# Two conditioned linear-attention layers: scores in column groups of 32, z on two engines, the output bias as a product

## The chip, the cores and the metric

The kernel runs on one core of a Trainium2 chip. The core has a matrix engine (PE in the profile; PEld is its loading of stationary operands), three engines that work on rows of 128 partitions (DVE, ACT, POOL) and a queue for transfers (SP; ACT issues some too). Each engine works through its own list of instructions in order, and the lists meet only at semaphores. The metric is the time of one execution on the device in microseconds (us), and of several executions the median.

## What is computed

Two layers, each on 16 sequences of 256 rows and 256 features. Layer 0 has 8 heads of 32 features and layer 1 has 16 heads of 16; they differ also in how a mask is applied. Cut to what matters, a layer is:

```python
xn = layernorm(x, w, b)
q = softmax(xn @ Wq + bq, over the features of a head)
k = softmax(xn @ Wk + bk + mask, over the 256 rows)
v = (xn @ Wv + bv) * mask
att = einsum('bnhd,bnhl->bhdl', k, v)        # a d x d block for each head: the "scores" of the kernel
y = einsum('bnhd,bhdl->bnhl', q, att)
h = layernorm(y) * (1 + scale) + shift       # scale and shift from the condition
x = x + silu(h) @ W_out + b_out
```

## The kernel before

**Tiling.** An item is one sequence of one layer, so there are 32 items, numbered through both layers. Rows lie on partitions: a sequence is a tile of 128 x 512 (T = 2 halves of 128 rows, each of 256 features), and features are cut into C = 2 chunks of 128. Pairs of buffers alternate by the item's parity.

**The stages of an item.**
- z: DVE takes mean and variance of x (`x_statistics`, `x_aggregate`), POOL the reciprocal root (`x_scale`), DVE writes z = (x - mean) * rstd in two halves of 128 x 256 (`x_normalise`, L933). ACT makes z_hi in 16 bits (L397), adding Z_SCALE as a bias, DVE the rest z_lo (L944). Two DMA transposes turn both.
- products: PE makes K transposed (`project_k`, L1375, 12 products of 256 columns) and Q and V (`project_qv`, L1395, 12 of 512 columns).
- softmax: DVE and ACT. exp(k) is turned on PE (L1409), exp(q) too (L1439).
- scores: `attend` (L1467). G = 64: for each chunk and half of the rows, two products of 128 rows with 64 x 64 columns in 32-bit floats, one for each half of the array's columns; 8 products an item. Off-diagonal head blocks come out too. `att_scale` (DVE, L1020 and L1022) multiplies them by `block_mask`, which sets them to zero.
- y: `attention_out` (L1483), 8 products an item with 64 rows each, 66 or 68 columns wide (the last column of each head gives the sum of exp(q)). DVE divides and takes statistics; POOL and ACT normalise one half each (L707, L469). PE turns the result (L1450), ACT conditions it (L483), ACT and DVE make silu in two 16-bit parts g_hi and g_lo (L505, L1094).
- out: `project_out` (L1428), 12 products of 256 columns. POOL has written x_plus = x + b_out (L719), and DVE adds the product to it and writes x (`residual`, L1102).

**Order.** Everything is written out by hand: each engine's function lists the stages of different items one after the other, with a loop for the middle of the program. In PE's loop one turn holds these stages, each of another item: y, scores, out, exp(q) turned, Q and V, exp(k) turned, y turned, K. A wait stands ahead of a stage where a buffer must be full or free.

**Tiles of the array.** A product is laid on a part of PE's array that its shape gives. The profile prints it as rows*columns: 128*128 for the projections, 64*128 for `attention_out`, 128*64 for `attend`.

## Time and profile before

| | us |
|---|---|
| median of 3 runs | 308.25 |
| lowest and highest of them | 308.12, 308.55 |
| the profiled execution, whole | 307.67 |
| its span, first to last instruction | 305.9 |
| PE busy | 287.3 |
| DVE busy | 281.4 |
| ACT busy | 234.2 |
| POOL busy | 152.7 |

The profile has a page and a trace. The page sums each engine's busy time and follows the chain of work that ended last backwards from the last instruction. The trace can be asked for the busy times in a stretch of the span, for groups of equal instructions, and for single instructions in order of time. A record of PE lasts longer than PE is held by it, because products run through the array one behind the other; what a product costs a full PE is the time from its start to the next start. The same holds for the other engines to a smaller degree. Products of 32-bit floats have two records each, the turns on PE one.

### The profile page before, as it was taken

What the parts mean: (1) busy time and instruction counts of PE and PEld (TensorE: products, weight loads), DVE (VectorE), ACT (ScalarE), POOL (GpSimd) and SP (SyncE); (2) the same over time, 40 slices, a digit from 0 to 9 for tenths busy, and PEclk for the clock granted to TensorE, in tenths of its full rate; (3) what the DMA queues carried; (4) which work ended last, traced back from release to release, by engine and by line L of the source; (5) the groups of instructions that cost most, each with busy time, mean ns of one, the idle gap of its engine ahead of it and who ended that gap; (6) DMA issues with size and microseconds to landing.
All of it is one profiled execution on the core that took longest, in us unless ns stands there. A gap on an engine that the chain in (4) does not pass through costs nothing.

```text
span 305.9 us, 8521 instructions
## 1 busy us (share of the span) xinstructions
PE 287.3 (94%) x2629; PEld 210.3 (69%) x2629; DVE 281.4 (92%) x850; ACT 234.2 (77%) x525; POOL 152.7 (50%) x268
## 2 busy tenths in 40 slices
PE   8388999999999999999999999999999999999665
PEld 3145666677777777777777777777777777777553
DVE  3967899999989999999999999999999999888985
ACT  1426347698998888888898989998889988888760
POOL 1220202335555555666655655555556665564774
PEclk9869999999999999999999999999999999999998
DMA  7499856553222222211221222232222222711224
GB/s 222 134 252 264 197 130 168 128 155 56 55 53 54 55 51 49 48 39 43 55 53 37 55 54 51 54 56 51 51 43 50 52 40 54 239 36 38 70 69 139
DMA packets 51485, 26.73 MB, mean 87 GB/s; under 512 B 36656, under 2 KB 49648, under 8 KB 51440
## 3 DMA queue, kind: packets, MB, share of 16 engines
q1 hardware_dynamic: 50000, 25.03, 33.6%
q10 hardware_dynamic: 1440, 1.15, 1.1%
q8 instruction: 22, 0.36, 0.5%
q14 instruction: 23, 0.19, 0.2%
HBM read 13.55 MB, written 4.23 MB: 58 GB/s over the span
## 4 chain that ended last, share of the span: by engine, by line
PE 85%; DVE 6%; DMA 3%; issue 2%; ACT 1%; ACTq 0%; SPq 0%; DVEq 0%
PE ps_qv L1395 25%; PE ps_eo L1428 14%; PE ps_k L1375 14%; PE ps_y L1483 11%; PE ps_att L1467 6%; PE ps_qy L1439 5%; PE ps_eo L1409 4%; PE ps_qy L1450 4%; DMA m1r<-in_mask_row 2%; DMA zt_hi<-z_hi 2%; PE ps_k L1428 1%; DVE w_raw L817 1%; DVE g_lo L1094 1%; PE ps_y L1333 1%; DVE z_lo L944 1%
## 5 line engine op out<-in xcount | busy, mean ns | idle before, releaser
L719 POOL TENSOR_TENSOR x_plus<-x_all,row_b 128x512 f32<-128x512 f32 x32 | 43.2, 1354 | 53.5 <-DVE x_all L1102 53.5
L1395 PE MATMUL ps_qv<-w_hi,zt_hi 128*128 128x512 f16 x128 | 49.0, 383 | 0.0
L1395 PE MATMUL ps_qv<-w_lo,zt_hi 128*128 128x512 f16 x128 | 48.9, 382 | 0.0
L1395 PE MATMUL ps_qv<-w_hi,zt_lo 128*128 128x512 f16 x128 | 48.8, 381 | 0.0
L679 POOL TENSOR_SCALAR x_ve<-x_mv 128x2 f32<-128x2 f32 x32 | 6.2, 193 | 75.5 <-DVE x_mv L921 75.3
L1375 PE MATMUL ps_k<-zt_hi,w_hi 128*128 128x256 f16 x128 | 35.4, 277 | 7.9 <-DVE w_lo L830 5.9
L1428 PE MATMUL ps_eo<-wo_hi,g_hi 128*128 128x256 f16 x120 | 33.4, 278 | 3.7 <-DVE x_all L1102 2.4
L1483 PEld LDWEIGHTS ps_y<-att_e,eq_t 64*128 64x128 f32 x512 | 31.1, 187 | 7.0 <-issue 7.0
L1483 PE MATMUL ps_y<-att_e,eq_t 64*128 64x66 f32 (+1 forms) x512 | 35.6, 278 | 0.3 <-DVE att_e L1022 0.3
L408 ACT ACTIVATE ek<-k_neg,k_neg_max 128x256 f32<-128x256 f32 x64 | 31.6, 497 | 5.1 <-DVE k_neg_max L956 5.1
L1375 PE MATMUL ps_k<-zt_hi,w_lo 128*128 128x256 f16 x128 | 35.5, 277 | 0.0
L1375 PE MATMUL ps_k<-zt_lo,w_hi 128*128 128x256 f16 x128 | 35.5, 277 | 0.0
L1094 DVE SCALAR_TENSOR_TENSOR g_lo<-g,g_hi 128x512 f16<-128x512 f32 x32 | 34.1, 1066 | 1.5 <-ACT g_hi L505 1.4
L483 ACT ACTIVATE h<-ps_qy,item_col 128x256 f32<-128x256 f32 x64 | 32.4, 558 | 3.0 <-DVE g L1085 2.4
L440 ACT ACTIVATE v<-ps_qv,item_col 128x256 f32<-128x256 f32 x64 | 29.6, 467 | 6.5 <-PE ps_qv L1395 5.4
L1428 PE MATMUL ps_eo<-wo_hi,g_lo 128*128 128x256 f16 x120 | 33.3, 277 | 0.0
L1428 PE MATMUL ps_eo<-wo_lo,g_hi 128*128 128x256 f16 x120 | 33.2, 276 | 0.0
L459 ACT ACTIVATE eq_t<-ps_qy 128x512 f32<-128x512 f32 x32 | 19.1, 596 | 18.0 <-PE ps_qy L1439 17.9
L397 ACT ACTIVATE z_hi<-z,z_plus 128x512 f16<-128x512 f32 x32 | 22.8, 714 | 5.5 <-DVE z L933 5.4
L450 ACT ACTIVATE eq<-q_sub 128x512 f32<-128x512 f32 x32 | 19.8, 620 | 8.5 <-DVE q_sub L1000 8.4
L1102 DVE SCALAR_TENSOR_TENSOR x_all<-ps_eo,x_plus 128x512 f32<-128x512 f32 x30 | 20.1, 669 | 5.5 <-PE ps_eo L1428 4.8
L990 DVE TENSOR_REDUCE q_max<-ps_qv 128x16 f32<-128x512 f32 (+1 forms) x32 | 21.1, 660 | 4.1 <-ACT v L440 4.1
(101 smaller groups left out, 755.1 us busy)
## 6 DMA issues: line engine op xcount, KB each, us to landing
m_row<-mask_rows SPq DMA_DIRECT2D x32, 128.0 KB, 3.3
out<-x_all SPq DMA_DIRECT2D x16, 256.0 KB, 2.2
wemb<-in_w_emb SPq DMA_DIRECT2D x2, 1024.0 KB, 7.1
w_raw<-in_w_in SPq DMA_DIRECT2D x2, 768.0 KB, 5.2
x_all<-in_x SPq DMA_DIRECT2D x3, 512.0 KB, 5.2
x_all<-in_x SPq DMA_DIRECT2D x2, 768.0 KB, 6.3
x_all<-in_x ACTq DMA_DIRECT2D x4, 256.0 KB, 5.9
row_b<-in_rows SPq DMA_DIRECT2D x2, 384.0 KB, 6.3
```

The costliest lines, as they stand in the source:

```text
L397: nc.scalar.activation(z_hi[p][:, :], z[p][:, :], ACT.Identity, bias=z_plus[:, 0:1]).then_inc(z_hi_ready, 1)
L408: last = nc.scalar.activation(part(ek[p], c), part(k_neg[p], c), ACT.Exp, scale=-1.0, bias=k_neg_max[p][:, c:c + 1], accum_out=k_sum[p][:, ...
L440: nc.scalar.activation(part(v[p], t), ps_qv[:, t * BANK + D:(t + 1) * BANK], ACT.Copy, scale=item_col[a.layer][:, m:m + 1]).then_inc(v_rea ...
L483: last = nc.scalar.activation(part(h[p], c), part(ps_qy, c), ACT.Identity, scale=item_col[a.layer][:, ab + 2 * c:ab + 2 * c + 1], bias=ite ...
L719: pool.tensor_tensor(x_plus[p][:, :].rearrange("p (t f) -> p t f", t=T), sequence_of(a).rearrange("p (t f) -> p t f", t=T), row_b[a.layer] ...
L990: vec.tensor_reduce(q_m, q, AX_X, ALU.max).then_inc(q_max_ready, 1)
L1094: vec.scalar_tensor_tensor(g_lo[p][:, :], g[p][:, :], G_SCALE, g_hi[p][:, :], ALU.mult, ALU.subtract)\
L1102: vec.scalar_tensor_tensor(sequence_of(a), out_bank(a)[:, :], 1.0 / OUT_SCALE, x_plus[p][:, :], ALU.mult, ALU.add).then_inc(x_new, 1)
L1375: last = mm(part(ps_k, d).rearrange("p (t s) -> p t s", t=T), w[l][:, c * W + d * P:c * W + (d + 1) * P], zz[p][:, :].rearrange("p (t c s) ...
L1395: last = mm(part(ps_qv, t, BANK), zz[p][:, (t * C + c) * P:(t * C + c + 1) * P], w[l][:, c * W + D:(c + 1) * W], start=(n == 0), stop=(n = ...
L1428: last = mm(part(out_bank(a), t), gg[p][:, c * S + t * P:c * S + (t + 1) * P], part(w[l], c), start=(n == 0), stop=(n == 3 * C - 1))
L1483: last = mm(ps_y[:, at:at + E], eq_t[p][r * G:(r + 1) * G, c * S + t * P:c * S + (t + 1) * P], att_e[l][p][r * G:(r + 1) * G, c * E:(c + 1 ...
```

## The change

- **Scores.** G becomes 32. `attend` makes 16 products of 32 x 32 columns, one for each quarter of the array's columns, in place of 8 of 64 x 64. `att_scale` writes each score block four times over, side by side, times a mask of 128 columns, so that att_e is a full 128 x 128 block diagonal per chunk (two instructions of 128 x 128 elements). `attention_out` then is 4 products of 128 rows and 132 or 136 columns in place of 8 of 64 rows and 66 or 68 columns, and y lies half by half.
- **z.** z = x * rstd + shift, with Z_SCALE inside the shift. DVE makes the first half, ACT the second. POOL's `x_scale_and_shift` has four small instructions in place of two. z_hi is a plain copy in 16 bits, z_lo a plain difference.
- **Bias.** x_plus and POOL's sum are gone. Each half of `project_out` begins with a product of 33 rows: row 0 of `bias_pair` holds b_out's high part, row 32 the low part, the rows between are zero. It starts the sum in PSUM, and the 6 products follow. `residual` adds to x itself.
- **Start.** The mask rows of items 0 and 1 are loaded straight from the input. Loads of x move from ACT's queue to SP's, `mask0_row` and `mask1_row` behind others on ACT's. PE begins with Q and V of item 0, then K. SP's waits for buffers are ordered anew, and stores stand in the loop.
- **Order.** The lists of all engines are written anew, with the same stages.

```diff
-    G = 64
-    GROUPS = P // G
-    GH = [G // d for d in DH]
+    HC = [P // d for d in DH]
+    G = 32
...
             load_sequence(0)
             load(ident[:, :], identity, ident_in)
+            load_sequence(1)
+            load(head_ind[:, :], indicators, ind_in)
             load(m0r[:, :], mask0_row, mask_in)
             load(m1r[:, :], mask1_row, mask_in)
-            load(head_ind[:, :], indicators, ind_in)
-            for b in range(1, 4):
-                load_sequence(b)
...
+            def x_normalise(a):
+
+                j, p = a.index, a.parity
+                act.wait_ge(x_shift_ready, j + 1)
+                if not a.first_two:
+
+                    act.wait_ge(z_lo_ready, j - 1)
+                nc.scalar.activation(part(z[p], 1), part(sequence_of(a), 1), ACT.Identity, scale=x_rstd[p][:, 1:2],
+                                     bias=x_shift[p][:, 1:2]).then_inc(z_ready[1], 1)
...
-                nc.scalar.activation(z_hi[p][:, :], z[p][:, :], ACT.Identity, bias=z_plus[:, 0:1]).then_inc(z_hi_ready, 1)
+                nc.scalar.activation(z_hi[p][:, :], z[p][:, :], ACT.Copy).then_inc(z_hi_ready, 1)
...
                 pool.tensor_scalar(x_ve[p][:, :], x_mv[p][:, 1:2 * T:2], Z_SCALE ** -2, EPS * Z_SCALE ** -2, ALU.mult, ALU.add)\
-                    .then_inc(x_ve_ready, 1)
-                pool.wait_ge(x_ve_ready, j + 1)
-                pool.tensor_tensor(x_rstd[p][:, :], x_ve[p][:, :], neg_half[:, :], ALU.pow).then_inc(x_rstd_ready, 1)
+                    .then_inc(x_powered, 1)
+                pool.wait_ge(x_powered, 3 * j + 1)
+                pool.tensor_tensor(x_rstd[p][:, :], x_ve[p][:, :], neg_half[:, :], ALU.pow).then_inc(x_powered, 1)
+                pool.wait_ge(x_powered, 3 * j + 2)
+                pool.tensor_tensor(x_nm[p][:, :], x_mv[p][:, 0:2 * T:2], x_rstd[p][:, :], ALU.mult).then_inc(x_powered, 1)
+                pool.wait_ge(x_powered, 3 * j + 3)
+                pool.tensor_scalar(x_shift[p][:, :], x_nm[p][:, :], -1.0, Z_SCALE, ALU.mult, ALU.add).then_inc(x_shift_ready, 1)
...
-            def add_out_bias(a):
...
-                pool.tensor_tensor(x_plus[p][:, :].rearrange("p (t f) -> p t f", t=T),
-                                   sequence_of(a).rearrange("p (t f) -> p t f", t=T),
-                                   row_b[a.layer][:, bo:bo + D].unsqueeze(1).to_broadcast([P, T, D]), ALU.add)\
-                    .then_inc(x_plus_ready, 1)
...
-                for t in range(T):
-                    last = vec.tensor_scalar(part(z[p], t), part(sequence_of(a), t), x_mv[p][:, 2 * t:2 * t + 1],
-                                             x_rstd[p][:, t:t + 1], ALU.subtract, ALU.mult)
-                last.then_inc(z_ready, 1)
+                vec.tensor_scalar(part(z[p], 0), part(sequence_of(a), 0), x_rstd[p][:, 0:1], x_shift[p][:, 0:1],
+                                  ALU.mult, ALU.add).then_inc(z_ready[0], 1)
...
+                for c in range(C):
+                    att = part(ps_att, c, G)
+                    if l == 0:
+                        last = vec.scalar_tensor_tensor(scaled[:, c], att.unsqueeze(1).to_broadcast([P, P // G, G]),
+                                                        k_rsum[p][:, c:c + 1], mask, ALU.mult, ALU.mult)
...
                 for t in range(T):
+                    here = part(out_bank(a), t)
+                    mm(here, bias_ones[:, :], bias_pair[l][:, :], start=True, stop=False)
                     n = 0
...
-                        for r in range(GROUPS):
+                        for r in range(P // G):
...
                 for t in range(T):
                     for c in range(C):
-                        for r in range(GROUPS):
-                            at = r * BANK + (t * C + c) * E
-                            last = mm(ps_y[:, at:at + E], eq_t[p][r * G:(r + 1) * G, c * S + t * P:c * S + (t + 1) * P],
-                                      att_e[l][p][r * G:(r + 1) * G, c * E:(c + 1) * E], start=True, stop=True)
+                        last = mm(ps_y[:, t * BANK + c * E:t * BANK + (c + 1) * E], eq_t[p][:, c * S + t * P:c * S + (t + 1) * P],
+                                  part(att_e[l][p], c, E), start=True, stop=True)
```

Where the instructions stand now is shown at two places of PE's list and one of POOL's. In a row stand the line, the operation, what it writes and reads, and the size of what it writes; x8 stands for so many alike in a row.

PE in the loop of layer 1, before: y of one item directly ahead of the scores of the next, and then the first half of an out product.

```order
L1375 MATMUL ps_k<-zt_hi,w_lo 128x256
L1483 MATMUL ps_y<-att_e_1,eq_t 128x66 x8
L1467 MATMUL ps_att<-ek_row,v 64x64 x8
L1428 MATMUL ps_eo<-wo_hi,g_hi 128x256
L1428 MATMUL ps_eo<-wo_lo,g_hi 128x256
```

Here `ps_eo` is the bank that out and the turned exp(k) share. PE after, the same stages: y, then out with its product of 33 rows (L1501) ahead of each half.

```order
L1515 MATMUL ps_qy<-ident,eq 128x128 x4
L1557 MATMUL ps_y<-att_e_1,eq_t 128x136 x4
L1501 MATMUL ps_eo<-bias_pair,bias_ones 128x256
L1506 MATMUL ps_eo<-wo_hi,g_hi 128x256
L1506 MATMUL ps_eo<-wo_lo,g_hi 128x256
L1506 MATMUL ps_eo<-wo_hi,g_lo 128x256
L1506 MATMUL ps_eo<-wo_hi,g_hi 128x256
L1506 MATMUL ps_eo<-wo_lo,g_hi 128x256
L1506 MATMUL ps_eo<-wo_hi,g_lo 128x256
L1501 MATMUL ps_eo<-bias_pair,bias_ones 128x256
L1506 MATMUL ps_eo<-wo_hi,g_hi 128x256
```

Y has moved away from the scores, and out has two products more. In the built program the tile of L1501 is 64*128, since 33 rows are more than 32 and at most 64; its neighbours on both sides are 128*128. PE after, at the end of the same turn of the loop, where the scores stand now, between K and the turned y.

```order
L1449 MATMUL ps_k<-zt_hi,w_lo 128x256
L1543 MATMUL ps_att<-ek_row,v 32x32 x16
L1526 MATMUL ps_qy<-ident,y_z 128x128 x4
L1469 MATMUL ps_qv<-w_hi,zt_hi 128x512
L1469 MATMUL ps_qv<-w_lo,zt_hi 128x512
```

The scores are the one stage left on 128*32 tiles; y is on 128*128 now.

POOL in the loop, before: one turn with x_plus (L719).

```order
L692 TENSOR_SCALAR y_ve<-y_mv 128x2
L693 TENSOR_SCALAR y_nm<-y_mv 128x2
L695 TENSOR_TENSOR y_rstd<-y_ve,neg_half 128x2
L697 TENSOR_TENSOR y_shift<-y_nm,y_rstd 128x2
L679 TENSOR_SCALAR x_ve<-x_mv 128x2
L682 TENSOR_TENSOR x_rstd<-x_ve,neg_half 128x2
L707 TENSOR_SCALAR y_z<-y_n,y_rstd,y_shift 128x2x2x64
L719 TENSOR_TENSOR x_plus<-x_all,row_b 128x512
```

POOL after: the same turn, with two small steps more for x and without the sum.

```order
L726 TENSOR_SCALAR y_ve<-y_mv 128x2
L727 TENSOR_SCALAR y_nm<-y_mv 128x2
L729 TENSOR_TENSOR y_rstd<-y_ve,neg_half 128x2
L731 TENSOR_TENSOR y_shift<-y_nm,y_rstd 128x2
L709 TENSOR_SCALAR x_ve<-x_mv 128x2
L712 TENSOR_TENSOR x_rstd<-x_ve,neg_half 128x2
L714 TENSOR_TENSOR x_nm<-x_mv,x_rstd 128x2
L716 TENSOR_SCALAR x_shift<-x_nm 128x2
L740 TENSOR_SCALAR y_z<-y_n,y_rstd,y_shift 128x256
```

POOL's only instruction of 128 x 512 has gone.

## Rows read from the trace of the kernel before

**Rows 1.** The page: span, busy times by engine, and the chain by engine.

```profile
span 305.9 us, 8521 instructions
PE 287.3 (94%) x2629; PEld 210.3 (69%) x2629; DVE 281.4 (92%) x850; ACT 234.2 (77%) x525; POOL 152.7 (50%) x268
PE 85%; DVE 6%; DMA 3%; issue 2%; ACT 1%; ACTq 0%; SPq 0%; DVEq 0%
```

**Rows 2.** Stretches: length, then busy time (instructions) of PE, PEld, DVE, ACT, POOL.

```profile
179.48:262.31 82.83, 82.83 (x801) 63.00 (x800) 81.05 (x236) 74.86 (x170) 47.47 (x78) 1.00 0.24 51
262.31:305.90 43.59, 34.88 (x321) 26.48 (x318) 35.88 (x73) 28.66 (x61) 27.39 (x39) 0.96 0.29 97
```

**Rows 3.** The chain in order of time (start, length): Q and V, ten turns apart.

```profile
179.48 2.59 PE ps_qv L1395 x12
...
262.31 2.59 PE ps_qv L1395 x12
```

**Rows 4.** PE in order of time (start, duration) across y, scores and out.

```profile
167.41 0.27 PE L1375 MATMUL ps_k<-zt_hi,w_lo 128*128 128x256 f16 x1
167.61 1.11 PE L1483 MATMUL ps_y<-att_e,eq_t 64*128 64x68 f32 x16
168.66 0.69 PE L1467 MATMUL ps_att<-ek_row,v 128*64 128x64 f32 x16
169.27 0.28 PE L1428 MATMUL ps_eo<-wo_hi,g_hi 128*128 128x256 f16 x1
169.39 0.27 PE L1428 MATMUL ps_eo<-wo_lo,g_hi 128*128 128x256 f16 x1
```

**Rows 5.** The same scores, the second and the third pair of records first.

```profile
168.76 0.58 PE L1467 MATMUL ps_att<-ek_row,v 128*64 128x64 f32 x14
...
168.82 0.52 PE L1467 MATMUL ps_att<-ek_row,v 128*64 128x64 f32 x12
```

**Rows 6.** PE at the start: 32-bit products on the whole array and on quarters.

```profile
7.66 0.61 PE L1312 MATMUL ps_y<-ident,kb 128*128 128x128 f32 x4
8.10 1.02 PE L1315 MATMUL ps_y<-w_raw,fold 128*128 128x512 f32 x2
...
39.29 0.38 PE L1395 MATMUL ps_qv<-w_hi,zt_lo 128*128 128x512 f16 x1
39.60 1.07 PE L1325 MATMUL ps_y<-wemb,cond_s 128*32 128x512 f32 x8
40.59 0.66 PE L1409 MATMUL ps_eo<-ident,ek 128*128 128x128 f32 x4
```

**Rows 7.** Groups by line, 179.48 to 262.31: count, busy us, mean ns, idle before.

```profile
L1094 DVE SCALAR_TENSOR_TENSOR g_lo<-g,g_hi 128x512 f16<-128x512 f32 x10 | 11.4, 1143 | 0.0
L944 DVE SCALAR_TENSOR_TENSOR z_lo<-z,z_hi 128x512 f16<-128x512 f32 x10 | 6.8, 677 | 0.0
L933 DVE TENSOR_SCALAR z<-x_all,x_mv,x_rstd 128x256 f32<-128x256 f32 x18 | 6.5, 402 | 0.0
L1022 DVE TENSOR_TENSOR att_e<-ps_att,block_mask 128x128 f32<-128x128 f32 x10 | 2.8, 277 | 0.0
...
L483 ACT ACTIVATE h<-ps_qy,item_col 128x256 f32<-128x256 f32 x20 | 10.2, 558 | 0.6 <-DVE g L1085 0.6
L397 ACT ACTIVATE z_hi<-z,z_plus 128x512 f16<-128x512 f32 x10 | 7.1, 713 | 0.0
```

**Rows 8.** Groups of the end, 262.31 to 305.9, and its longest wait of PE.

```profile
L1094 DVE SCALAR_TENSOR_TENSOR g_lo<-g,g_hi 128x512 f16<-128x512 f32 x10 | 10.2, 1031 | 1.5 <-ACT g_hi L505 1.4
L1085 DVE SCALAR_TENSOR_TENSOR g<-th,h 128x512 f32<-128x512 f32 x9 | 7.6, 851 | 0.0
...
PE ps_eo L1428 <- DVE x_all L1102: 2.4, 1, 2.4
```

**Rows 9.** DVE and POOL in order of time, one turn of the loop.

```profile
204.79 1.27 POOL L719 TENSOR_TENSOR x_plus<-x_all,row_b 128x512 f32<-128x512 f32 x1 [2.15 <-DVE x_all L1102]
...
205.39 1.22 DVE L1094 SCALAR_TENSOR_TENSOR g_lo<-g,g_hi 128x512 f16<-128x512 f32 x1
```

920 lines of the change are left out of this document (527 added, 393 removed).

## The prediction

> **What bounds the kernel now.** I read four views in this order: the page, a table of stretches, the chain in order of time, and single instructions of one turn of the loop. The page gives a span of 305.9 us with PE busy 94% and 85% of the last chain on PE [rows 1]. Busy shares alone can't separate PE from DVE (92%), so I take one stretch in which the loop repeats. From 179.48 to 262.31, ten turns, PE has no idle time at all: 82.83 us busy of 82.83. DVE has 81.05 and ACT 74.86 [rows 2]. The chain confirms it: Q and V start at both ends of the stretch [rows 3]. A turn, one item, is therefore 82.83 / 10 = 8.28 us, set by the sum of PE's starts. DVE is close behind with 8.11, so taking work from DVE or POOL alone gains nothing here, while each 0.1 us more on PE costs 3.2 us over 32 items. The end, from 262.31 on, is different: PE is busy 34.88 of 43.59 us [rows 2], and waits once 2.4 us for DVE [rows 8]. There a faster DVE can pay.
>
> **What PE pays now for y and scores.** The last K product starts at 167.41 and the first out product at 169.27 [rows 4]. That is 1.86 us, less 0.11 for the K product itself (169.39 less 169.27 is 0.12 for such a product, of 256 columns in 16 bits, straight after a change of tile): 1.75 us. In it are three gaps where the tile's shape changes: 128*128 to 64*128 takes 167.61 - 167.41 - 0.11 = 0.09 us on top of the product. The scores' first step takes 168.76 - 168.66 = 0.10 us, later steps 168.82 - 168.76 = 0.06 [rows 4, 5], so a 32-bit load after a change costs 0.04 more. From 168.76 six steps of 0.06 lead to the last pair at 169.12 or a little less, its own step ends at 169.17, and out starts at 169.27: the change back costs 0.10. In each step of the scores two records start, one for each half of the array's columns.
>
> **Y after.** Four products of 128 rows, 136 columns in layer 1 and 132 in layer 0, two records each, so eight steps. A 32-bit record of 128 columns on the whole array takes (8.10 - 7.66) / 4 = 0.11 us [rows 6], so these take 0.117 and 0.113: 0.92 us an item. No change of shape stands beside them now.
>
> **Scores after.** Entry 0.09, first load 0.04 to 0.05, eight steps of four records, exit 0.10. The trace has no product this small on quarters, so a step is bounded from both sides. Low: four quarter tiles run at once, and a step is half of 0.06 because the columns are half as many. That four do run at once is in the trace: eight records of 512 columns on 128*32 tiles take 40.59 - 39.60 = 0.99 us [rows 6], where one such record takes 4 x 0.11 = 0.44 us; in fours they need 0.88 and one change. High: PE is held to the number of records, now 0.03 us each, so a step of four takes 0.12. I take the geometric middle, 0.06, which is also the nearest row's own step. Scores: 0.09 + 0.05 + 0.48 + 0.10 = 0.72 us (0.48 to 1.20). Y and scores together: 1.64 us for 1.75, a gain of 0.11 (a gain of 0.35 to a loss of 0.37).
>
> **The bias.** Two products of 256 columns in 16 bits an item: 2 x 0.11 = 0.22 us. Each is on a 64*128 tile between neighbours on 128*128, so out has four changes of shape. A change costs 0.09 on the way to 64*128 and 0.10 on the way back [rows 4]: 0.40 us. Together 0.62 us. The bounds are 0.22, if such a product runs through without a gap, and 0.80, if each of the two also pays the 32-bit load of 0.04 and the product behind it too. I take 0.62, since the row shows the very same pair of shapes.
>
> **PE an item:** +0.62 - 0.11 = +0.51 us, over 32 items +16.3 us (+0.27 to +0.99, that is +9 to +32).
>
> **DVE, POOL, ACT.** POOL's x_plus (1.27 us) runs beside g_lo, and g_lo then takes 1.22 us [rows 9] where an instruction of the same form and size takes 0.68 [rows 7]. Without x_plus DVE regains (1.143 - 0.677) = 0.47 us an item, and half of z, at most 0.40. It pays one more att_e instruction, at most 0.28 [rows 7]. DVE ends near 8.11 - 0.47 - 0.40 + 0.28 = 7.5 us a turn, under PE. In the loop this gain is hidden by PE and worth nothing. ACT gets half of z, at most 0.56 by the row of h [rows 7], on 7.49 busy a turn: about 8.0, under PE's 8.8. POOL has two small steps more and a big one less (4.75 us busy a turn): slack. The new waits on POOL and ACT (for x_shift) hold back z of an item that PE wants a turn and more later. Behind ACT's wait stand h and the turned exp(k); z's statistics were taken some ten DVE instructions earlier, so I cost it at nothing; without that cover it is POOL's two steps, under 1 us, once.
>
> **End.** Ten g_lo of 1.031 and nine g of 0.851 [rows 8] against 0.677 make 3.5 + 1.6 = 5.1 us of DVE; I count 3 of them on the path. PE's extra time in out is in the sum for these items too (ten of them, 6.2 us), but PE is idle 8.7 us there [rows 2], so I take back 1.5.
>
> **Start.** POOL's two extra steps and DVE's wait for a mask load that stands two places further back delay the first z; item 0 and 1's masks no longer pass through DRAM. I cost it at +1 us (-1 to +3); PE's first wait is for weights, which DVE makes in both kernels.
>
> **Sum** on the profiled execution: 307.67 + 16.3 - 3 - 1.5 + 1 = 320.5 us. The median of the runs shown is 0.58 us above that execution: **321 us**.
>
> **Rivals.**
> A. *The product of 33 rows runs without a gap, and the four quarters stream at once.* PE then changes by 0.22 - 0.35 = -0.13 us an item, -4 us; with 3 us from the end the kernel comes to 301, or with the middle price of the scores (+0.11, +3.5 us) to 309. For it: with 64 rows left idle, the hardware might treat rows as masked. Against it: the gap of 0.09 before y is a change of exactly these two shapes. It decides as soon as a bias product with its two changes costs under 0.11 us each. This is the faster side. The Trainium skill, TensorEngine Tiling, Key Properties, says that changing the tiling mode drains TensorE; by this rule A cannot be, and the trace's gaps at all three changes agree (0.09 to 0.10 us). It is the rule that speaks most against this change.
> B. *The scores are held to the number of records.* A step is 0.12, the scores 1.20 us, +0.99 us an item: 307.67 + 31.7 - 3.5 + 0.6 = about 336. For it: a turn now has 32 records in a row that do little work each. Against it: two records start together in each step, and the eight big ones on quarters overlap. The same page, Instruction Overhead, states about 60 cycles for each matmul, so that few columns cost as much as 60; by an estimate from it at 2.4 GHz (25 ns a record) the scores take 0.80 us plus 0.24 and the kernel comes to 331. No run shown here has such a product.
> C. *Another engine sets the turn.* ACT at 8.0 us, if an order of stages makes it wait 0.8 us or more for PE every turn, would stretch the turn beyond 8.8. Its lists are new and this can't be read from the trace: 2 to 6 us more, 325.
>
> **Chances.** Forecast (scores low to middle, four gaps; 311 to 329) 0.62. A 0.17, of which 0.13 falls below the old time, 0.02 beside it and 0.02 above. B 0.15. C 0.06. A measurement can tell 0.2% (0.6 us) from no change; faster 0.14, same 0.03, slower 0.83. The range is 307 to 334: it leaves out most of A's faster side (0.12) and the far end of B (0.07).
>
> **What would show it.** In the loop: turns of about 8.8 us with PE without idle time; four gaps of about 0.09 us in out, around each product of the bias; scores of about 0.7 us with four starts close together; y in 0.92 us; g_lo at about 0.68 us; DVE idle about 1 us a turn, waiting for PE. A is right if the bias product follows after 0.11 us. B is right if the scores take over 1 us. The forecast is wrong altogether if PE has idle time in the loop, since then another engine or an order sets the turn, or if the start is off by more than 3 us.

## The result, and the profile after

| | before | after |
|---|---|---|
| median (lowest to highest), 4 runs each on one chip | 308.19 (307.65 to 308.55) | 313.88 (313.43 to 314.3) |
| profiled execution, span | 307.67, 305.9 | 313.51, 311.7 |
| PE busy, span less PE busy | 287.3, 18.6 | 293.9, 17.8 |
| a turn of the loop, layer 0 and layer 1 | 8.28, 8.28 | 8.60, 8.62 |

The change makes the kernel slower by 5.7 us: ratio 1.0186, 95% interval 1.0162 to 1.021. The direction is the predicted one; the forecast was 12.8 us, more than twice as much. Now and then an execution takes far longer than the others of the same program, also of the kernel before (1005.68 us once, 584 us in two of the four of e8b_sum_beside, 341 us at a granted clock of 0.841 in one of e6_one_bias and one of e15_scores_bias33), for reasons that are open; the ratios leave these out.

The page of the kernel after: span, busy times, and the granted clock in 40 slices. It answers to [rows 1].

```profile
span 311.7 us, 9221 instructions
...
PE 293.9 (94%) x2949; PEld 205.6 (66%) x2949; DVE 269.5 (86%) x846; ACT 240.4 (77%) x557; POOL 117.2 (38%) x300
...
PEclk9859999999999999999999999999999999999999
```

PE's busy time grew by 6.6 us and DVE's fell by 11.9. The time outside PE's work hardly changed (18.6 and 17.8 us).

Stretches, with columns as in [rows 2] (length, then busy time and count of PE, PEld, DVE, ACT, POOL, then granted clock, DMA share, GB/s). First the kernel before, then after.

```profile
0.00:80.00 80.00, 70.08 (x550) 45.19 (x551) 66.86 (x246) 44.92 (x103) 22.24 (x59) 0.96 0.66 166
80.00:260.00 180.00, 180.00 (x1736) 136.61 (x1736) 177.85 (x531) 159.01 (x358) 103.04 (x171) 1.00 0.23 49
...
280.00:300.00 20.00, 15.05 (x134) 11.75 (x133) 17.73 (x31) 13.36 (x26) 15.47 (x21) 0.92 0.18 61
```

```profile
0.00:80.00 80.00, 66.31 (x581) 42.62 (x581) 65.16 (x237) 46.64 (x111) 27.78 (x79) 0.94 0.69 163
80.00:260.00 180.00, 180.00 (x1885) 129.69 (x1884) 165.00 (x510) 157.08 (x369) 74.69 (x190) 1.00 0.25 51
...
280.00:300.00 20.00, 19.34 (x196) 13.38 (x195) 16.93 (x46) 16.82 (x36) 8.66 (x18) 1.00 0.16 54
```

From 80 to 260 us PE has no idle time in either kernel, so PE sets the turn in both, and DVE has gained slack (165.00 for 177.85). Up to 80 us PE is idle for 9.9 us before and 13.7 after: here the turn isn't PE's alone. At 280 to 300 us PE stood still a quarter of the time before, and the granted clock was 0.92 on the mean: part of the stretch, behind those pauses, at the lower level of 1.2 GHz. After, PE is busy 19.34 of 20 us and the clock stays at 1.00, the level of 2.4 GHz.

What the lower level cost the kernel before can be read from its last chain (start, length), where each row is the twelve products of one item's out:

```profile
291.25 1.49 PE ps_eo L1428 x12
292.74 1.32 PE ps_k L1428 x12
...
296.55 2.55 PE ps_eo L1428 x12
299.10 1.90 PE ps_k L1428 x12
```

From 294 to 297 us PE was busy for 1.12 us, and from 297 to 300 the granted clock was 0.50. The two pairs of rows differ by (2.55 - 1.49) + (1.90 - 1.32) = 1.6 us. The kernel after has no such stretch between 262 us and its last product.

One turn of PE after, in order of time (start, duration): K's last product, the scores, the turned y, one Q/V product, then y, and out with its two bias products. It answers to [rows 4, 5].

```profile
183.12 0.27 PE L1449 MATMUL ps_k<-zt_hi,w_lo 128*128 128x256 f16 x1
183.32 0.46 PE L1543 MATMUL ps_att<-ek_row,v 128*32 128x32 f32 x32
183.71 0.66 PE L1526 MATMUL ps_qy<-ident,y_z 128*128 128x128 f32 x4
184.21 0.38 PE L1469 MATMUL ps_qv<-w_hi,zt_hi 128*128 128x512 f16 x1
...
187.67 1.09 PE L1557 MATMUL ps_y<-att_e,eq_t 128*128 128x136 f32 x8
188.69 0.28 PE L1501 MATMUL ps_eo<-bias_pair,bias_ones 33*128 33x256 f16 x1
...
189.46 0.27 PE L1506 MATMUL ps_eo<-wo_hi,g_lo 128*128 128x256 f16 x1
189.67 0.28 PE L1501 MATMUL ps_eo<-bias_pair,bias_ones 33*128 33x256 f16 x1
189.88 0.28 PE L1506 MATMUL ps_eo<-wo_hi,g_hi 128*128 128x256 f16 x1
```

Read the starts, as ahead. A full product of 256 columns takes 0.11. Into the bias product: 189.67 - 189.46 = 0.21, that is 0.10 more. Out of it: 189.88 - 189.67 = 0.21, again 0.10 more. So the four gaps of the prediction are there, in their size. (The profile prints the bias product's tile as 33*128, by its rows.) Y takes 188.69 - 187.67 = 1.02, of which 0.09 is the first gap: 0.93. The scores' 32 records start at 183.32 and the next tile at 183.71: 0.39 us, with the exit. Less 0.10 for it and 0.04 for the first load, eight steps take 0.25, 0.03 each: half of the old step, the low bound of the prediction. Entry is 0.09, and the four turned y take 0.50 where four such take 0.44 at the start (8.10 - 7.66, [rows 6]): 0.06 for a first load behind the scores.

To see where the time went I cut each profile at three starts on PE: the first Q product of item 8, that of item 28, and the last item's first product with W in out. Times in us from the span's start; the lengths between them stand beside.

| kernel | item 8 | to item 28 (20 turns) | to last out | that start |
|---|---|---|---|---|
| before | 79.94 | 165.64 | 55.52 | 301.10 |
| after | 80.96 | 172.21 | 53.41 | 306.58 |
| difference | +1.02 | +6.57 | -2.11 | +5.48 |

The rows of the last two marks, before and then after:

```profile
245.58 0.38 PE L1395 MATMUL ps_qv<-w_hi,zt_hi 128*128 128x512 f16 x1
...
301.10 0.27 PE L1428 MATMUL ps_eo<-wo_hi,g_hi 128*128 128x256 f16 x1
```

```profile
253.17 0.38 PE L1469 MATMUL ps_qv<-w_hi,zt_hi 128*128 128x512 f16 x1
...
306.58 0.28 PE L1506 MATMUL ps_eo<-wo_hi,g_hi 128*128 128x256 f16 x1
```

The loss is made in the loop, 20 turns of +0.33 us. The prediction's sum put 20 x 0.51 = 10.2 there. These marks are those of one execution each. The place of item 8 scatters: in e8c_sum_ahead, which differs from the kernel after only by a sum that first runs at 95.80 us, item 8 starts at 85.02.

### The profile page after: what moved, and what is told of

The parts are those of the page before. It is cut to its first block, busy times and chain, and to the rows that moved or that the text cites. A ratio compares the mean times of both kernels' runs of the same rounds, so it can differ in the third digit from the quotient of the medians.

```text
span 311.7 us, 9221 instructions
## 1 busy us (share of the span) xinstructions
PE 293.9 (94%) x2949; PEld 205.6 (66%) x2949; DVE 269.5 (86%) x846; ACT 240.4 (77%) x557; POOL 117.2 (38%) x300
## 4 chain that ended last, share of the span: by engine, by line
PE 77%; DVE 3%; DMA 2%; issue 2%; ACT 1%; SPq 0%; DVEq 0%; ACTq 0%
PE ps_qv L1469 22%; PE ps_eo L1506 14%; PE ps_k L1449 11%; PE ps_y L1557 9%; PE ps_qy L1526 5%; PE ps_qy L1515 4%; PE ps_eo L1483 4%; PE ps_eo L1501 4%; PE ps_att L1543 4%; DMA zt_hi<-z_hi 2%; DVE g L1114 1%; DVE x_all L1130 0%; ACT h L463 0%; DVE g_lo L1123 0%; DVE q_max L1014 0%
## 5 line engine op out<-in xcount | busy, mean ns | idle before, releaser
L709 POOL TENSOR_SCALAR x_ve<-x_mv 128x2 f32<-128x2 f32 x32 | 14.3, 446 | 130.6 <-DVE x_mv L946 130.4
L1557 PE MATMUL ps_y<-att_e,eq_t 128*128 128x132 f32 (+1 forms) x256 | 34.7, 278 | 0.0
L1130 DVE SCALAR_TENSOR_TENSOR x_all<-ps_eo,x_all 128x512 f32<-128x512 f32 x30 | 20.5, 682 | 16.3 <-PE ps_eo L1506 16.1
L1557 PEld LDWEIGHTS ps_y<-att_e,eq_t 128*128 128x128 f32 x256 | 31.7, 190 | 0.4
L421 ACT ACTIVATE v<-ps_qv,item_col 128x256 f32<-128x256 f32 x64 | 27.6, 470 | 5.5 <-PE ps_qv L1469 5.5
L409 ACT ACTIVATE ek_row<-ps_eo 128x512 f32<-128x512 f32 x32 | 19.0, 595 | 14.3 <-PE ps_eo L1483 14.3
L366 ACT ACTIVATE z<-x_all,x_shift,x_rstd 128x256 f32<-128x256 f32 x32 | 19.0, 594 | 12.6 <-POOL x_shift L716 12.6
L1469 PEld LDWEIGHTS ps_qv<-w_hi,zt_hi 128*128 128x128 f16 x128 | 12.7, 99 | 20.9 <-issue 12.6
L980 DVE CUSTOM_DVE_ANT_0 k_neg<-ps_k,m_row 128x256 f32<-128x256 f32 x64 | 24.3, 417 | 0.0
L485 ACT ACTIVATE g_hi<-g 128x512 f16<-128x512 f32 x32 | 20.1, 629 | 5.4 <-issue 3.3
```

Source lines behind the costliest of these rows:

```text
L366: nc.scalar.activation(part(z[p], 1), part(sequence_of(a), 1), ACT.Identity, scale=x_rstd[p][:, 1:2], bias=x_shift[p][:, 1:2]).then_inc(z_ ...
L421: nc.scalar.activation(part(v[p], t), ps_qv[:, t * BANK + D:(t + 1) * BANK], ACT.Copy, scale=item_col[a.layer][:, m:m + 1]).then_inc(v_rea ...
L485: nc.scalar.activation(g_hi[p][:, :], g[p][:, :], ACT.Copy, scale=G_SCALE).then_inc(g_hi_ready, 1)
L980: last = vec.tensor_tensor_reduce(out=part(k_neg[p], c), in0=part(ps_k, c), in1=m_row[p][:, :], scale=-1.0 / QKV_SCALE, scalar=BIG, op0=AL ...
L1130: vec.scalar_tensor_tensor(sequence_of(a), out_bank(a)[:, :], 1.0 / OUT_SCALE, sequence_of(a), ALU.mult, ALU.add).then_inc(x_new, 1)
L1469: last = mm(part(ps_qv, t, BANK), zz[p][:, (t * C + c) * P:(t * C + c + 1) * P], w[l][:, c * W + D:(c + 1) * W], start=(n == 0), stop=(n = ...
```

## The experiments

Theory D: the loss is the changes of tile shape around the bias products, about 0.10 us each. Theory P: what is won back in the end comes from POOL's sum being gone. The expectations, quoted as they were written ahead of each run, name the rivals. Each run has a label, given at its edit and shortened later (e1 for e1_pad128). Times are medians; ratios are to the kernel before on the same chip.

### The bias product on full rows

Run e1_pad128. In place of 33 rows, 128, of which rows 1 to 31 and 33 to 127 are zero: same columns, same number of products, no change of shape.

```diff
-        bias_pair = [sb(f"bias_pair{l}", [GAP + 1, D], F16) for l in range(L)]
-        bias_ones = sb("bias_ones", [GAP + 1, P], F16)
+        bias_pair = [sb(f"bias_pair{l}", [P, D], F16) for l in range(L)]
+        bias_ones = sb("bias_ones", [P, P], F16)
```

> The changed kernel with the bias product made 128 rows tall (rows without bias are zero), so that it lies on a 128*128 tile like its neighbours; nothing else differs, and the result is the same. Theory D (each change of the tile's shape holds PE for about 0.10 us): the four gaps of a turn vanish, the turn falls from 8.62 to 8.22 us, and the kernel from 313.9 to about 301 us. Rival R (the product that starts a sum in PSUM costs 0.2 us whatever its rows): the turn stays at 8.6 and the time at 313 to 314 us.

Measured: 303.03 us (301.65 to 303.74), ratio 0.982 (0.9786 to 0.9853). PE in order of time around the bias:

```profile
184.03 1.09 PE L1557 MATMUL ps_y<-att_e,eq_t 128*128 128x136 f32 x8
184.96 0.27 PE L1501 MATMUL ps_eo<-bias_pair,bias_ones 128*128 128x256 f16 x1
185.07 0.27 PE L1506 MATMUL ps_eo<-wo_hi,g_hi 128*128 128x256 f16 x1
```

Y now takes 0.93 and the bias product 0.11. The turn falls from 8.60 to 8.18, by 0.42, or 0.105 for each of the four gaps. Ninety-five rows of zeros cost nothing and save 11 us: the slowdown by the change becomes a gain of 1.8%. D stands, and rival R falls: the product that starts a sum costs 0.11 us like any other.

### One bias product for both halves

Runs e6_one_bias and e6b_one_bias, of one kernel. One product of 33 rows and 512 columns for the whole bank, in place of two of 256. Columns stay, two of the four gaps go.

```diff
+                mm(out_bank(a)[:, :], bias_ones[:, :], bias_pair[l][:, :], start=True, stop=False)
                 for t in range(T):
                     here = part(out_bank(a), t)
-                    mm(here, bias_ones[:, :], bias_pair[l][:, :], start=True, stop=False)
```

> The changed kernel with one bias product of 33 rows and 512 columns for the whole bank in place of two of 256: the product's columns stay, the changes of tile shape go from four to two. Theory D (each change costs 0.10 us of TensorE wherever it stands): turn 8.60 - 0.20 = 8.40, time 313.9 - 32 x 0.20 = 307.5 (306 to 309). Rival F (the cost lies in the products of 33 rows themselves, not in the change): the same columns, hence turn 8.60 and 313 to 315. Rival G (cost per instruction): one instruction fewer, at most 0.03 a turn, 313.

Measured: 309.66 us, ratio 1.0042 (1.0026 to 1.0057), between the expectations. The turn is read in the second run of the same kernel.

> The kernel of e6_one_bias again (one bias product of 33 rows and 512 columns), for a profile at the full clock. From 309.7 instead of 313.9 us its turn should be 8.60 - 4.2/32 = 8.47. Theory D at 0.10 a change wants 8.40 to 8.42 in the turn, with the rest of the time lost at the start or the end. Rival D2 (a change back is cheaper or dearer where the product before is longer: 0.06 to 0.07 for each change taken out here) wants 8.46 to 8.48.

Measured: 309.98 us, ratio 1.0039 (1.0017 to 1.0062); turn 8.386 in layer 0 and 8.405 in layer 1, that is 0.213 less than after, 0.107 for each gap taken out. D holds in the turn, and the rivals F, G and D2 fall. The edit halves the number of 33-row products too, so a fixed price of 0.2 us for each of them would show the same; it is the next run, with two such products and only three new gaps, that speaks against it. Of the 6.8 us that this makes over 32 turns only 3.9 show in the median. The profile puts 2.3 of the rest ahead of item 8, which starts at 83.29, later by that than in the kernel after; there PE waits for a weight load (waits of PE from 26 to 48 us):

```profile
PE ps_y L1401 <- DMA wemb<-in_w_emb: 1.0, 1, 1.0
```

The kernel after has no such wait there. Why the load comes later is not settled.

### The bias product alone, without the scores and z

Run e2_bias33: the kernel before, with its bias as two products of 33 rows, POOL's sum and x_plus gone.

```diff
-                if s >= 9:
-                    add_out_bias(item(s - 9))
...
+                    mm(here, bias_ones[:, :], bias_pair[l][:, :], start=True, stop=False)
```

> The kernel before with one part of the change alone: the bias as a product of 33 rows, and POOL's sum gone. Theory D: the turn grows by 0.62 us to 8.90. If the end got shorter because POOL's sum no longer slows DVE (theory P), some 5 to 8 us come back there: 308.2 + 19.8 - 5 to 8 = 320 to 323 us. If the end got shorter through the new order (rival O), nothing comes back: 326 to 328 us.

Measured: 319.41 us, ratio 1.0361 (1.0332 to 1.039); turn 8.81, +0.53. PE in order of time:

```profile
183.89 0.69 PE L1462 MATMUL ps_att<-ek_row,v 128*64 128x64 f32 x16
184.51 0.28 PE L1420 MATMUL ps_eo<-bias_pair,bias_ones 33*128 33x256 f16 x1
184.72 0.28 PE L1425 MATMUL ps_eo<-wo_hi,g_hi 128*128 128x256 f16 x1
```

The first bias product follows the scores directly, where a gap stood anyway. So only three gaps are added: 0.22 + 3 x 0.10 = 0.52, as measured; a fixed 0.2 us for each product of 33 rows would make 0.62. 32 turns would make 17.0 us and 11.1 are there (the kernel before had 308.30 on that chip): 5.9 us come back outside the loop's turns, the amount that theory P wanted, but not all where it wanted it. By the profiled executions 3.1 us of it lie ahead of item 8 (8 x 0.53 = 4.2 us of PE's work, item 8 only 1.1 later, at 81.04). From item 28's Q to the last out 4 x 0.53 = 2.1 us of work are added and the stretch is 0.2 shorter, 55.30: 2.3 us for P.

Run e10_b_bias128: the same with products of 128 rows:

```diff
-        bias_pair = [sb(f"bias_pair{l}", [GAP + 1, D], F16) for l in range(L)]
+        bias_pair = [sb(f"bias_pair{l}", [P, D], F16) for l in range(L)]
```

> The kernel before with the bias as two products of 128 rows and 256 columns, POOL's sum gone; scores and z as before. Theory D (only the changes of tile shape beyond the products' own 0.107 us cost): no change is added behind the scores (128*64 to 128*128 was there), so the turn is 8.28 + 0.21 = 8.50, 0.32 less than e2_bias33's 8.81; with e2_bias33's gain of 5.9 us outside the turns the time is 308.3 + 7.0 - 5.9 = 309.4 (308 to 311). Rival E (the gain in e2_bias33's end was only cover for its longer products, worth less here): 312 to 315.

Measured: 310.8 us, ratio 1.0058 (1.0037 to 1.0079); turn 8.50, +0.22. That is the price of the columns alone. 32 turns make 7.0 us and 1.9 are there (the kernel before had 308.88 on that chip): 5.1 us come back, with no gap added. E falls, and the time is near the top of D's range. Item 8 starts at 81.05, as in e2 (81.04), though each item costs PE 0.31 us less: up to item 8 the time isn't set by what an item costs PE. From item 28's Q to the last out it takes 53.13.

### The scores alone

Run e3_scores32: the kernel before with `attend`, `att_scale`, `attention_out` and what prepares them from the changed kernel; bias on POOL, z on DVE.

```diff
-    G = 64
+    G = 32
```

> The kernel before with the other part alone: scores in column groups of 32 and y in four products, the bias still on POOL, the order as it was. By PE alone (rival) the turn falls by 0.28 us to 8.00 and the time to 299 us. Theory V: DVE, busy 8.11 us of a turn and now with 0.2 us more in att_e, sets the turn: 8.2 to 8.35 us, 307 to 309 us, and PE shows idle time in the loop.

Measured: 303.11 us, ratio 0.9829 (0.9804 to 0.9854); turns of 8.02 on the mean from item 8 to 16 (layer 0) and 8.15 from 16 to 28 (layer 1), with 7.92 for the first of them. DVE over 100 to 260 us is busy all the time, PE is not:

```profile
100.00:260.00 160.00, 158.91 (x1744) 119.80 (x1732) 160.00 (x490) 140.26 (x325) 94.50 (x156) 1.00 0.25 53
```

PE alone would turn in 7.92, 0.36 less than before. DVE holds the kernel back, since it pays for one more att_e while POOL's sum still makes g_lo long (1.09 us on the mean from 140 to 260 us). So the two ends of the expectation are both half right. The scores are the change's best part, and the forecast took them, with y, for a gain of 0.11 us.

### The bias back on POOL

Run e4_bias_pool: the changed kernel without bias products; POOL writes x_plus for item s - 11 at the end of its turn s.

```diff
-                    mm(here, bias_ones[:, :], bias_pair[l][:, :], start=True, stop=False)
...
                 normalise_y(item(s - 7))
+                if s >= 11:
+                    add_out_bias(item(s - 11))
```

> The changed kernel with the bias given back to POOL (x_plus by POOL's sum, no product for it); scores, z and orders as changed. Theory: PE's turn is 8.62 - 0.62 = 8.00 us; DVE has 7.5 + 0.5 (g_lo slowed by the sum) = 8.0 us, so the turn is 8.0 to 8.2. The end loses what it won from the missing sum. 313.9 - 19.8 + 5 to 8 = 299 to 302 us. If the order of stages held the changed kernel (rival), little comes back: over 306 us.

Measured: 318.53 us, ratio 1.0343 (1.0299 to 1.0387), a miss by 17 us, in the rival's range (over 306). Its waits from 100 to 260 us (us in total, times, longest):

```profile
DVE x_all L1151 <- POOL x_plus L754: 17.3, 18, 1.1
```

DVE comes to x_all 0.96 us on the mean before POOL's sum is done, and the next out's load on PE waits for DVE (9.3 us in all, 17 times). My place for the sum was too late; the run says nothing on the bias. Once more, as e4b_bias_pool, one turn earlier and ahead of `normalise_y`:

```diff
-                if s >= 11:
-                    add_out_bias(item(s - 11))
+                if 10 <= s < 34:
+                    add_out_bias(item(s - 10))
                 normalise_y(item(s - 7))
```

> The changed kernel with the bias back in POOL's sum, as in e4_bias_pool, but with each item's sum one turn earlier and ahead of POOL's normalise_y, so that it doesn't come after DVE wants it. Theory D+M (in e4_bias_pool the missing 15 us were the wait of DVE for POOL's sum): TensorE's turn without bias products is 8.60 - 0.62 = 7.98, DVE's work 7.85, so the turn is 7.98 to 8.05 and the time 296 to 299. Rival L (POOL's sum in this kernel always ends last on the way of x, wherever it stands, or slows DVE beside it): DVE waits for x_plus or is busy all the time, turn 8.15 or more, time 301 or more.

Measured: 305.23 us (303.78 to 306.94), ratio 0.988 (0.9827 to 0.9934): above D's range and in rival L's (301 or more). In layer 1 the turn is 8.00, as D says (8.60 - 0.62 = 7.98). In layer 0 turns vary from 7.97 to 9.35, 8.41 on the mean, as L says: now `normalise_y` comes 1.27 us later, and DVE's y_n waits for y_z (3.8 us, seven times). Item 8's Q starts at 84.20, 3.2 us later than after. With the start put in order (below), as e12_pool_start:

> e4b_bias_pool with the start of e5_pad_start and e7_start (which took 1.6 us off the changed kernel and 2.1 us off the one padded to 128 rows). If e4b_bias_pool gives 296 to 299, this gives 1.5 to 2 less, 294.5 to 297, the lowest of all. If e4b_bias_pool's turn is 8.15 or more, 299.5 or more, near e5_pad_start's 301.0.

Measured: 302.36 us, ratio 0.9784 (0.9744 to 0.9823), 2.9 us less than e4b. So POOL can carry the bias at a PE turn of 8.0 in layer 1. The whole is no better than the full-row product with the same start (e5_pad_start, 300.96, below): the 20 turns from item 8 to 28 take 163.29 us against 163.81 there, and the stretch from item 28's Q to the last out 51.99 against 50.27. What PE gains is lost in layer 0's turns and in the end.

### The start

Run e7_start: the changed kernel with DVE's mask rows and value masks behind the first key weights, POOL's copy of the indicators behind its third item, and the mask rows' transfer behind item 0's. Run e5_pad_start has the same and the padding of e1.

```diff
-            mask_rows()
             x_statistics(item(1))
-            value_masks()
             x_aggregate(item(1))
...
             k_weights(0)
+            mask_rows()
+            value_masks()
```

> The changed kernel with the start put in order as in e5_pad_start, and nothing else. Theory S: first projection at 16 to 17 us instead of 19.21, the turn stays at 8.60, the time 313.9 - 2 to 3 = 311 to 312. Rival H: 19 to 20 us, 313 to 315. With e1_pad128 and e5_pad_start it tells whether the two gains add.

> The changed kernel with the bias product's operands padded to 128 rows (as in e1_pad128) and with the start put in order: DVE's mask rows and value masks behind item 0's key weights, POOL's indicator copy behind its third x_scale_and_shift, and the mask rows' transfer behind item 0's turns. Theory S (the start's loss is a wait of DVE for the mask load and of POOL for head_ind, ahead of the first z): TensorE's first projection comes at 16 to 17 us instead of 19.90, the turn stays at 8.18 to 8.20, and the time is 303.0 - 3 to 4 = 299 to 300.5. Rival H (the start is set by a transfer of weights that all the start's work waits for, w_lo): first projection still at 19 to 20 us, time 302 to 304.

Measured: 312.34 us (ratio 1.0139, 1.0122 to 1.0156) and, with the padding of e1, 300.96 us (0.9774, 0.9759 to 0.9788). That is 1.5 and 2.1 us less than without (medians, not all taken on one chip; the executions of e7, 312.3 to 312.7, and those of the kernel after don't overlap). Three long waits up to 20 us in the kernel after, and the first product of Q in after and in e7:

```profile
PE ps_qv L1469 <- DVE w_lo L863: 9.6, 1, 9.6
POOL att_e L697 <- DMA head_ind<-in_indicators: 9.3, 1, 9.3
DVE m_add L782 <- DMA m1r<-in_mask_row: 5.7, 1, 5.7
```

```profile
19.21 0.58 PE L1469 MATMUL ps_qv<-w_hi,zt_hi 128*128 128x512 f16 x1 [9.56 <-DVE w_lo L863]
```

```profile
17.50 0.59 PE L1469 MATMUL ps_qv<-w_hi,zt_hi 128*128 128x512 f16 x1 [7.76 <-DVE w_lo L863]
```

DVE and POOL stood behind two loads that nobody needed yet. S holds in direction, H falls; PE's first product moved by 1.7 us, to 17.50 rather than 16 to 17, item 8's Q by 0.8, to 80.15, and both times are a little above S's ranges.

### Without the z split and the new orders

Scores and bias of the changed kernel on the kernel before: z on DVE alone, every engine's order and the start as before. Once with 128 rows (e14_scores_pad), once with 33 (e15_scores_bias33). The edits are those of the scores alone and of the bias alone, together:

```diff
-    G = 64
+    G = 32
...
-                if s >= 9:
-                    add_out_bias(item(s - 9))
...
+                    mm(here, bias_ones[:, :], bias_pair[l][:, :], start=True, stop=False)
```

> The kernel before with scores in groups of 32 and the bias as two products of 128 rows, POOL's sum gone; z on DVE alone, the orders and the start as before. TensorE's turn should be e1_pad128's 8.18 to 8.20. Theory Z0 (the z split and the changed orders bring nothing at this turn): e10_b_bias128's 310.8 - 32 x 0.31 = 300.9, less a little for the start: 299 to 301.5, below e1_pad128's 303.0. Theory Z (the z split relieves DVE where it is needed): turn over 8.25 or a longer end, 303 or more.

> As e14_scores_pad, with the products of 33 rows: the change without its z split, its new orders and its start. TensorE's turn should be the changed kernel's 8.60. Theory Z0: e2_bias33's 319.4 - 32 x 0.21 = 312.7, 311.5 to 313.5. Theory Z: 315 to 317, since the changed kernel has 313.9 in spite of a first projection 3.3 us later.

Measured: 299.62 us, ratio 0.9712 (0.967 to 0.9755), the fastest kernel of this case; and 309.12 us, ratio 1.0018 (0.9997 to 1.0038), which can't be told from the kernel before. The first is in Z0's range. The 33-row kernel is 4.8 us faster than the changed one and below both expectations. Its turn in layer 0 is 8.446, not 8.60. PE in order of time:

```profile
186.67 0.46 PE L1455 MATMUL ps_att<-ek_row,v 128*32 128x32 f32 x32
187.06 0.28 PE L1413 MATMUL ps_eo<-bias_pair,bias_ones 33*128 33x256 f16 x1
```

Here y, scores and bias stand in a row (y starts at 185.65): the exit from the scores is also the entry to the bias. In the changed kernel's order the scores stand between K and the turned y: one gap more (0.09) and the first load behind them (0.06) make 0.15, and 8.60 - 8.45 = 0.15. So the new order of PE itself costs 0.15 us a turn, 3.0 us over the 20 turns from item 8 to 28, of 4.2 between the two profiled executions. Another 1.5 lie ahead of item 8 (79.46 for 80.96), where e15 has the start of the kernel before, and the end gives 0.3 back (53.71 for 53.41). With 128 rows only the load is left: 8.135 against 8.179. In the turn, which PE sets, the z split brings nothing; in the end and the start it wasn't separated from the new orders.

The marks of the table above, for three kernels:

| kernel | item 8 | to item 28 | to last out |
|---|---|---|---|
| scores alone, bias on POOL | 78.19 | 161.88 | 55.38 |
| scores, bias in 128 rows | 78.96 | 162.98 | 50.69 |
| the same in 33 rows | 79.46 | 169.20 | 53.71 |

The first two lines differ in nothing but the bias' way. Taking it off POOL shortens the end by 4.7 us, though PE has 0.22 us more work an item. That shows P's place and size.

### Why the end is shorter: POOL's sum beside DVE

The last chain in order of time (start, length) of the scores alone, with x_plus on POOL:

```profile
276.65 1.27 POOL x_plus L708
...
280.80 1.28 POOL x_plus L708
282.54 1.75 DVE g L1078
...
285.60 2.74 PE ps_eo L1421 x12
...
289.50 1.27 DVE g_lo L1087
290.81 1.36 DVE g_lo L1087
...
294.33 0.99 DVE g_lo L1087
```

and of the kernel with the bias in 128 rows, where POOL is not in the end's chain at all and each such DVE instruction takes 0.60 to 0.70:

```profile
279.12 0.60 DVE g_lo L1079
...
291.68 0.70 DVE g_lo L1079
```

POOL's sums are twice in the chain themselves (2.55 us), and four DVE instructions are together 2.65 us longer than 0.68 each (1.75 + 1.27 + 1.36 + 0.99 - 4 x 0.68 = 2.65). A third part is PE's clock: behind a pause the granted clock is 0.50 here from 286 to 288 us, and out's twelve products take 2.74 us, where e14's, with two of the bias more, take 1.53 (284.93 to 286.46) at 1.00. The parts make more than the 4.7 us, so they don't all add. Three kernels look at the second part. Each adds to the changed kernel a POOL sum of 128 x 512 numbers a turn that nobody reads: extra work, nothing left out.

```diff
+                pool.tensor_tensor(x_plus[a.parity][:, :], row_b[1][:, 0:N], row_b[1][:, D:D + N], ALU.add).then_inc(aside, 1)
```

Run e8_sum_aside, at the end of POOL's turn:

> The changed kernel with an additional POOL sum of 128 rows and 512 columns of 32-bit numbers in each turn from item 0 on, whose result nobody reads and for which nobody waits: POOL's old work as a load on the memory alone. Theory P (POOL's sum slows DVE's vector work beside it, and this is why the old end was longer): in the loop DVE's g_lo goes from 0.66 back to near 1.1 us, the turn stays near 8.6 since TensorE sets it, and the end grows by 3 to 6 us: time 317 to 320. Rival O (the old end was long by its order and its waits, not by the load): g_lo may be slower but the end is unchanged, 313 to 315.

Measured: 317.02 us, ratio 1.0299 (1.0271 to 1.0326). The end grows from 53.41 to 55.35, 1.9 us, at a granted clock of 1.00 throughout. The rest is ahead of the loop: item 8 starts at 82.93, 2.0 us later, but the first added sum starts only at 89.33, so that this part isn't the sum's. In the loop g_lo stayed at 0.66: there the sum ran beside q_sub and x_all, which take one operand from PSUM, and neither changed (0.68). In the end's chain, where sums pile up, g_lo and g are long again:

```profile
303.43 1.69 DVE g_lo L1137
...
306.79 1.69 DVE g L1128
```

So not any sum beside any DVE instruction. In e8b_sum_beside the sum stood right behind DVE's aggregate of x's statistics, where g_lo runs:

```diff
+                    pool.tensor_tensor(x_plus[p][:, :], row_b[0][:, 0:N], row_b[0][:, D:D + N], ALU.add).then_inc(aside, 1)
                 pool.tensor_scalar(x_ve[p][:, :], x_mv[p][:, 1:2 * T:2], Z_SCALE ** -2, EPS * Z_SCALE ** -2, ALU.mult, ALU.add)\
```

> The changed kernel with an additional, unread POOL sum of 128 rows and 512 columns in each turn from item 9 on, as in e8_sum_aside, but in the place right behind DVE's aggregate of x's statistics, where DVE's g_lo runs. In e8_sum_aside the sum stood beside q_sub and x_all, whose durations didn't change (0.68, 0.68). Theory P2 (the slowing is between POOL's sum and g_lo, SBUF to SBUF, when they run together): g_lo goes from 0.66 to about 1.1 us in the loop, DVE's work to 8.3, the turn stays 8.60 to 8.65. Theory P0 (no slowing from POOL's sum at all; g_lo was slow in the kernel before for another reason): g_lo stays 0.66. Time in both: 313.9 + 0 to 2, as the last sums end with item 31's x and the end is free of them.

Measured: 316.81 and 317.39 us, and twice 584; no ratio is formed, and the trace is that of the 317.39. One turn of both engines:

```profile
181.97 1.64 POOL L716 TENSOR_TENSOR x_plus<-row_b 128x512 f32<-128x512 f32 x1 [3.27 <-DVE x_mv L954]
...
181.81 0.65 DVE L1131 SCALAR_TENSOR_TENSOR g_lo<-g,g_hi 128x512 f16<-128x512 f32 x1
```

Neither theory: g_lo keeps its 0.65 us, but POOL's sum takes 1.64 instead of 1.27. g_lo had started 0.16 us earlier. In [rows 9] it was the other way round: the sum started first and g_lo was long. The third kernel, e8c_sum_ahead, lets DVE's k_neg release POOL's sum, ahead of g_lo:

```diff
+                    pool.wait_ge(k_neg_ready, j - 2)
...
+                    pool.tensor_tensor(x_plus[p][:, :], row_b[0][:, 0:N], row_b[0][:, D:D + N], ALU.add).then_inc(aside, 1)
```

> The changed kernel with an unread POOL sum of 128 rows and 512 columns in each turn from item 12 on, now released by DVE's k_neg, so that POOL's sum is under way or first in line when DVE comes to g_lo. In e8b_sum_beside g_lo came first, by 0.16 us: it kept 0.66 us and POOL's sum took 1.64 instead of 1.27. Theory X (the two exclude each other, and the one that started first ends first): g_lo takes 1.1 to 1.9 us, ending about 0.55 us behind the sum; DVE's work of a turn goes from 7.85 to 8.3 to 9.0, and if over 8.60 the turn goes with it: time 314 to 322. Rival W (POOL is the one that always gives way): g_lo stays 0.66, POOL's sum 1.6, time 314 to 316.

Measured: 314.13 us (312.91 to 317.55), ratio 1.0197 (1.0127 to 1.0267). One turn, and g_lo's group over 100 to 260 us:

```profile
173.71 1.66 POOL L712 TENSOR_TENSOR x_plus<-row_b 128x512 f32<-128x512 f32 x1 [2.59 <-DVE k_neg_max L989]
...
173.56 0.68 DVE L1123 SCALAR_TENSOR_TENSOR g<-th,h 128x512 f32<-128x512 f32 x1
...
174.32 1.60 DVE L1132 SCALAR_TENSOR_TENSOR g_lo<-g,g_hi 128x512 f16<-128x512 f32 x1
```

```profile
L1132 DVE SCALAR_TENSOR_TENSOR g_lo<-g,g_hi 128x512 f16<-128x512 f32 x18 | 28.9, 1604 | 0.0
```

Theory X holds, in one turn both ways: g was first and kept 0.68, the sum behind it was stretched to 1.66; then the sum was first and g_lo had to wait, ending at 175.92, 0.55 us behind the sum's end at 175.37. The Trainium skill, SBUF — State Buffer, section "SBUF: two separate sides", says this of a DVE instruction with two SBUF inputs and a POOL instruction that reads SBUF: they share a port pair under an exclusive lock, and whichever starts first has it for its whole length. These runs agree, and so does the 0.68 us of q_sub, which has one operand in PSUM, beside the sum in e8. DVE's busy time rose to 159.31 of 160 us, its slack was just enough, and PE's turn stayed at 8.60: in the loop the cost is hidden. In the end of e8 it isn't.

## Why the prediction was right, and where it was wrong

The direction and what makes it were right: PE sets the turn, and the bias products cost it more than scores and y give back. The size was not, 12.8 us for 5.7. Three steps failed: the price of the scores, the count of items that pay PE's price, and the end, whose relief was put too high and left out the clock.

- **PE bounds the loop, before and after.** Right: 180.00 us of 180 in both. Rival C's waits of ACT did not come.
- **The bias, +0.62 us an item.** Right to 0.02: four gaps of 0.10 to 0.107 and 0.22 for the columns. Two edits that take gaps out, e1 (0.42 for four) and e6b (0.213 for two), and e10 (0.22 for the columns) show each part. The Trainium skill's rule that a change of tiling mode drains TensorE (TensorEngine Tiling, Key Properties) holds here at 33 rows too, with 0.10 us for each change. Rival A fails at its condition; without the gaps its time is reached (303.03, within its 301 to 309).
- **Y, 0.92.** Right: 0.93 in layer 1.
- **The scores, 0.72 us: the first wrong step.** The middle of 0.48 to 1.20 was chosen since the old step was 0.06. The step is 0.03, and the scores take 0.09 + 0.39 + 0.06 = 0.54. The term is 0.18 too big, 5.8 us over 32 items. The row of eight records of 512 columns on quarters [rows 6] had said that four quarters run at once, and the old step of 0.06 for two halves of 64 columns is what two full-speed halves need: a record's cost went by its columns, and there was no row for a floor. I let a floor that no row showed pull the estimate up. Rival B fails, at both its prices: 32 records start in less than 0.39 us, not in 0.96 or 0.80.
- **PE an item, +0.51 times 32: the second wrong step.** Measured +0.33. And not every item pays it. Up to item 8 PE is idle 9.9 of 80 us, and there +8 x 0.33 = 2.6 us of work came with +1.0 us of time, a later start included. The same in e2, +8 x 0.53 = 4.2 us of work and +1.1 of time, and in e10, +1.8 and +1.1. The prediction gave the end a share of its idle time back (1.5 us) and the beginning nothing.
- **The end, -4.5: the third wrong step.** With the measured turn the sum makes 4 x 0.33 - 4.5 = -3.2 from item 28's Q on; measured -2.1 up to the last out and +0.3 behind it, -1.8: 3.1 us came back. The reason was right, but part of it: DVE's long g_lo and g come from POOL's sum, by exclusion and not by a general slowing, and POOL's sum was itself in e3's chain. The clock had no term, though [rows 2] showed 0.96 for this stretch: 1.6 us of PE's time at the lower level are gone with the pauses ahead of it. How the 3.1 us divide between DVE's instructions and the clock isn't separated. The whole is 4.7 us in e14 against e3, where one out alone takes 1.53 for 2.74 us.
- **DVE at 7.5 us a turn.** Measured 165.00 / 180 of 8.6, 7.9. g_lo is at 0.66 as said, and the relief was worth nothing in the loop, as said.
- **The start, +1 (-1 to +3).** PE's first product came 3.3 us later than before, at 19.21 instead of 15.88; Q of item 8 was 1.0 us later. The wait of DVE for the mask load (5.7 us) was seen, POOL's for the indicators (9.3 us) was not named. Putting both right brings 1.5 to 2.1 us. That item 8 came out at the forecast's +1 is partly luck, since its place scatters by more than that between nearly equal kernels.
- **The chances.** Slower at 0.83 doesn't follow from its parts: 0.62 + 0.15 + 0.06 and A's 0.02 make 0.85. Nothing hangs on it.
- **The order of PE's steps** was counted at nothing. It isn't: against y, scores, bias in a row it costs 0.15 us a turn. The forecast had it in its six gaps without seeing that one could be saved.

Together, in us: 12.8 forecast; the scores -5.8; the beginning -2.6 (8 x 0.33 + 1 = 3.6 in the sum, 1.0 measured); the end +1.4. That makes 5.8, and the profiled executions differ by 5.84.

## What to carry to other kernels

Where PE has no idle time, count changes of tile shape before columns: each cost 0.10 us here, so a small product should take its neighbours' shape, with rows of zeros if need be, or stand next to a product whose shape changes anyway. Multiply a turn's cost only by the turns in which that engine has no idle time. Moving a sum off POOL can pay twice, since it also stops holding up DVE's instructions with two SBUF operands; look which of the two starts first. Where PE pauses near the end, read the granted clock before giving the whole of a relief to one cause.
